# Two graph layers on one core: a pause in the first gathers, weight stages later, six last rows in one root

## The chip, the cores and the metric

The kernel runs on one core of one Trainium2 chip. The metric is the device time of one launch in microseconds (us), the median of several runs. TensorE multiplies and transposes, VectorE, ScalarE and GpSimd compute on tiles, SyncE issues most of the transfers, and GpSimd issues the indirect ones (gathers and scatters by an index column).

## What is computed

`x` is 50000 x 256 in float32. There are 12500 edges `(src, dst)`, sorted by `dst`. Two attention layers follow one another, each with a residual sum and a layer norm:

```python
x = layernorm(x + L0(x, edges))
x = layernorm(x + L1(x, edge_attr, edges))

# L0: 4 heads of 64
h = x @ W
e = leaky(h[src] @ a_src + h[dst] @ a_dst)
alpha = softmax of e over the edges with one dst
out = segment_sum(alpha * h[src], dst) @ W_out

# L1: 4 heads of 32
m = x @ W_n2m.T;  q, k, v from m;  e from edge_attr
alpha = softmax of q[dst] . (k[src] + e) over one dst
out = segment_sum(alpha * (v[src] + e), dst)
x_r = m @ Wskip.T + bskip
beta = sigmoid([out, x_r, out - x_r] @ Wbeta.T)
out = (beta * x_r + (1 - beta) * out) @ W_m2n.T
```

Most nodes have no incoming edge. For them both layers reduce to a function of their own row.

## The kernel before

The program has two kinds of work. **Node steps** (`Nodes`, 196 tiles of 256 rows) treat every row as if it had no edge: load, statistics, first norm, transpose (L741), product with the folded weights `m_ext` (L751), gated update (L777), squares (L716), root on GpSimd (L673, L678), final scaling (`Nodes.scale`: L688 on VectorE or L690 on ScalarE) and store (L658). **Edge work** goes over 100 tiles of 125 edges in five passes: `Score` gathers the rows of src and dst (L831) and projects them (L854 transposes, L864 and L866 products), `soft1` is a softmax over segments, `Gather` sums messages, `Message` builds keys, values and scores of the second layer, `soft2` is its softmax, and `Output` sums the second messages, applies the gate and the norm and scatters the rows over the output.

**Order of the work.** There is one plan, a list of pairs (part, step). Every engine goes through the same list and emits its own instructions of each pair, so each engine's queue is in the order of the plan. `order_of` blends the parts: node steps are spread over the passes by `NODE_SHARE`. `start_of` places the weight stages (`MADE_AT`), the mask stages (`MASKS_AT`) and the positions before given score tiles. In the plan before, node steps 187, 189, 191 and 193 lie among the last message tiles. Step 195 comes before soft2 1, 197 before soft2 4, 199 and 200 between soft2 9 and 10, 201 before soft2 11 and 203 before soft2 14. Node step s holds the scaling of node tile s - 8.

**Start.** `Weights` folds the weight matrices in stages 0 to 4: stage 1 transposes them (TensorE L294 to L297, VectorE L344 to L359), stage 2 multiplies them (L304 to L306, VectorE L363 to L367), stage 3 forms `m_ext` (L310, L311, L371 to L373) and stage 4 removes the means (L315 to L319, L378 to L392). `weights.pe_done` counts the stages that TensorE has finished. Stages 0 and 1 stand ahead of all score steps, stage 2 before score tile 1, stage 3 before tile 2, stage 4 before tile 4. The first mask stage (L449 to L461) stands before tile 1. A node tile is transposed only when stage 4 has made `m_ext` ready. GpSimd issues the two gathers of tile n at plan step n - 5, into a ring of 10 tiles, so it can run ahead of TensorE.

**Output.** Step t turns row tile t (`turn`, L1615), forms its skip product (`skip`, L1622, two tiles later), transposes the message of tile t (L1640), scans it on VectorE (L1712) and multiplies (L1644). The first two row tiles are turned early: tile 0 at t = -3, and at t = -2 come skip 0, turn 1 and skip 1, while the softmax still runs. VectorE finishes a row (L1690, L1702), ScalarE squares it (L1674), VectorE adds epsilon (L1716), GpSimd takes the power -0.5 (L1583), ScalarE scales (L1678) and GpSimd scatters (L1577). `GROUPS` says how many row tiles share one root: two, but one at either end. The tables `WIDENED_AT`, `ROOTS_AT`, `SCALED_AT` and `SCATTERED_AT` are worked out from it.

Of the kernel before, what the change touches and what calls it, by code (L numbers as in the profile page):

```python
# [35 lines left out]
EDGES, TILES = 125, 100  # L36
# [7 lines left out]
NSTEPS = NFULL + 1  # L44
# [5 lines left out]
def at_least(eng, sem, value):  # L50

    if value > 0:
        eng.wait_ge(sem, value)
# [24 lines left out]
def live(s, lag, total):  # L78

    return 0 <= s - lag < total  # L80
# [77 lines left out]
class Head:  # L158
# [53 lines left out]
    def pool(self, pool):  # L212
        c, w = self.c, self.c.scratch
        own = Own(pool, self.pool_done)
        own(pool.memset(c.ident[:, :], 0.0))
        own.done()
        own(pool.affine_select(out=c.ident[:, :], in_=c.ident[:, :], compare_op=ALU.not_equal, fill=1.0,
                               base=0, pattern=[[-1, P]], channel_multiplier=1))
        own(pool.memset(w.zero, 0.0))
        own(pool.memset(w.mean_w, 1.0 / D))  # L220
        own(pool.memset(c.half[:, :], -0.5))
        own(pool.memset(c.half_row[:, :], -0.5))
        own(pool.memset(c.we2[:, :, :], 0.0))
        own(pool.iota(w.posi, [[1, EDGES]], base=1, channel_multiplier=P))
        own(pool.iota(w.basei, [[1, 1]], base=0, channel_multiplier=P))
        own(pool.iota(w.placei, [[1, EDGES]], base=1, channel_multiplier=0))
        own(pool.iota(c.own_pos[:, :], [[P, TILES]], base=0, channel_multiplier=1))
        own.done()
        assert own.n == self.POOL_DONE
        pool.wait_ge(self.columns, 2)  # L230
# [16 lines left out]
    def tensor(self, pe):  # L247
        c, w = self.c, self.c.scratch
        pe.wait_ge(self.pool_done, 2)
        pe.wait_ge(self.dve_done, 7)  # L250
        for k in range(2):
            last = pe.transpose(c.psum[:, 0, k * 256:k * 256 + TILES], w.row[:, k, :], c.ident[0:TILES, 0:TILES])
        last.then_inc(self.turned, 1)


class Weights:

    FIRST, LAST = 0, 5
# [139 lines left out]
class Masks:  # L398

    FIRST, LAST = 0, 5  # L400
# [90 lines left out]
class Positions:  # L491

    FIRST, LAST = 0, 4
# [87 lines left out]
class Nodes:  # L581
# [3 lines left out]
    FIRST, LAST = 0, NSTEPS + 9  # L585
# [212 lines left out]
class Score:  # L798

    A = 5  # L800
    FIRST, LAST = -5, TILES + 2
# [20 lines left out]
    def pool(self, pool):  # L822
        c, R = self.c, self.c.R

        def emit(t):
            if live(t, -self.A, TILES):
                n = t + self.A
                at_least(pool, self.turned, n - R + 1)
                at_least(pool, self.kept[n % R], 16 * (n // R))
                for side, col in ((1, c.src_col), (0, c.dst_col)):  # L830
                    pool.indirect_dma_start(out=c.ring[:, n % R, side, :], out_offset=None, in_=self.x,  # L831
                                            in_offset=bass.IndirectOffsetOnAxis(ap=col[:, n:n + 1], axis=0)).then_inc(self.gathered[n % R], 16)
        return emit
# [62 lines left out]
class Finder:  # L896
# [3 lines left out]
    FIRST, LAST = 0, TILES // 4 + 1  # L900
# [98 lines left out]
class Softmax:  # L999

    PARTS = (0, 10, 40, TILES)
    FIRST, LATER, LAST = 0, 17, 19
# [178 lines left out]
class Gather:  # L1181

    A = 4
    FIRST, LAST = -4, TILES + 5
# [100 lines left out]
class Message:  # L1285

    A = 7
    B = 4
    PICKED = 5
    FIRST, LAST = -8, TILES + 3  # L1290
# [218 lines left out]
        return emit  # L1509


GROUPS = (1, 1) + (2,) * 48 + (1, 1)
GROUP_AT = [sum(GROUPS[:g]) for g in range(len(GROUPS) + 1)]
GROUP_OF = [g for g, size in enumerate(GROUPS) for _ in range(size)]
WIDENED_AT, ROOTS_AT, SCALED_AT, SCATTERED_AT = {}, {}, {}, {}
_at = 0
for _g, _size in enumerate(GROUPS):
    _last = GROUP_AT[_g] + _size - 1
# [8 lines left out]
class Output:  # L1527

    A = 5
    HELD = 10  # L1530
    EARLY = 4
    FIRST_ROWS = 2
    FIRST, LAST = -5, TILES + 11
    PAIRS = ((0, 1), (2, 3), (7, 4))

    def __init__(self, nc, c, ctx, out, masks, nodes, message, weights):
        self.c, self.out, self.masks, self.nodes, self.message, self.weights = c, out, masks, nodes, message, weights

        def sb(name, shape, dt=F32):
            return ctx.enter_context(nc.sbuf_tensor("output_" + name, shape, dt))  # L1540
# [9 lines left out]
        self.ZT = c.AT_flat[:, 0:4 * D].rearrange("p (a n) -> p a n", a=4)  # L1550
        self.va = sb("va", [P, 3, max(GROUPS)])
        self.r = sb("r", [P, 3, max(GROUPS)])
        self.rows_in = c.ring_load + c.ring_out
# [14 lines left out]
    def pool(self, pool):  # L1568
        c = self.c

        def emit(t):
# [7 lines left out]
            for g in ROOTS_AT.get(t, ()):  # L1579
                size = GROUPS[g]  # L1580
                pool.wait_ge(self.widened, g + 1)
# [26 lines left out]
    def tensor(self, pe):  # L1608
        c, ps = self.c, self.c.psum

        def turn(n):
            pe.wait_ge(self.rows_in[n % self.M], self.rows_before[n % self.M] + 16 * (n // self.M + 1))
            at_least(pe, self.zt_ready, n)
            for h in range(2):
                last = pe.transpose(ps[:, 6, h * P:(h + 1) * P], self.row(n)[:, h * P:(h + 1) * P], c.ident[:, :])  # L1615
            last.then_inc(self.z_turned, 1)

        def skip(n):
            pe.wait_ge(self.zt_ready, n + 1)
            at_least(pe, self.z_ready, n - 2)  # L1620
            for h in range(2):
                last = pe.matmul(ps[:, self.PAIRS[n % 3][1], 0:D + 1], self.ZT[:, n % 4, h * P:(h + 1) * P], c.m_ext[:, h, :], start=(h == 0), stop=(h == 1))  # L1622
            last.then_inc(self.skipped, 1)

        def emit(t):
            if t == -3:
                turn(0)
            if t == -2:
                pe.wait_ge(self.nodes.updated, NSTEPS)
                skip(0)  # L1630
                turn(1)
                skip(1)
            if live(t, 0, TILES) and t >= self.FIRST_ROWS:
                turn(t)
            if live(t, 2, TILES) and t - 2 >= self.FIRST_ROWS:
                skip(t - 2)
            if live(t, 0, TILES):
                pe.wait_ge(self.made, t + 1)
                at_least(pe, self.scanned, t)
                pe.transpose(ps[:, 5, 0:P], c.MSG[:, t % G, 0:DM], c.ident[:, :]).then_inc(self.turned, 1)  # L1640
            if live(t, 2, TILES):
                n = t - 2
                pe.wait_ge(self.scanned, n + 1)
                pe.matmul(ps[:, self.PAIRS[n % 3][0], 0:D + 3], self.AG[:, n % 5, :], c.w_out1[:, :], start=True, stop=True).then_inc(self.product, 1)  # L1644
        return emit
# [74 lines left out]
def main_pass(nc, c, io, out):  # L1720

    with ExitStack() as ctx:
# [10 lines left out]
        positions = Positions(nc, c, ctx, masks)  # L1733
        nodes = Nodes(nc, c, ctx, io["x"], out, made, NODE_NORMED, NODE_SCALED)
        assert TILES % c.R == 0
# [49 lines left out]

NODE_SHARE = (74, 10, 66, 45, 10)
NODE_NORMED = ["A" if 74 <= s < 84 or s >= 186 else "AD"[s % 2] if s >= 84 else "D" for s in range(NSTEPS)]
NODE_SCALED = ["AD"[s % 2] if s < 66 else "A" for s in range(NSTEPS)]

MESSAGES_BEGIN = ((3, 1), (1, 1), (1, 1), (1, 1))  # L1790

# [32 lines left out]
    return plan  # L1824


MADE_AT = (-5, -5, 1, 2, 4)
MASKS_AT = (1, 6, 8, 10, 12)
POSITIONS_AT = (14, 16, 18, 20)
NODES_FROM, FINDER_FROM = 2, 22  # L1830
# [2 lines left out]
def start_of(score, finder, nodes, made, masks, positions):  # L1833


    before = {}
    for at, part in ((MADE_AT, made), (MASKS_AT, masks), (POSITIONS_AT, positions)):
        for t, entry in zip(at, part):
# [106 lines left out]
```

## Time and profile before

| | us |
|---|---|
| median of 3 runs | 1260.95 |
| lowest and highest | 1257.87, 1261.74 |
| the profiled execution | 1271.05 |
| its span, first to last instruction | 1269.3 |
| busy in it: TensorE, VectorE | 1174.8, 1041.8 |
| busy in it: ScalarE, GpSimd | 829.2, 851.0 |
| mean granted TensorE clock | 0.978 |

The span is one traced execution, the median is of runs without a trace. The profiled execution is 10.1 us longer than the median. In the rows PE is TensorE, DVE VectorE, ACT ScalarE, POOL GpSimd and SP SyncE; a q behind the name is the engine's sequencer, which issues transfers. L12 is line 12 of the kernel. Matmuls overlap in their pipeline and their ends are modelled.

### The profile page before, as it was taken

Reading aid. Unit: us, or ns where it says so; the run is one execution under the profiler, and the core shown is the slowest. Engines: PE = TensorE matmul, PEld = TensorE weight load, DVE = VectorE, ACT = ScalarE, POOL = GpSimd, SP = SyncE. Lnnn points to the kernel's source line nnn. Section 1 sums busy time; section 2 is a strip of 40 time slices with the busy share of each in tenths; the row PEclk is TensorE's granted clock in tenths of the full one; section 3 lists DMA queues with packets and bytes.
Section 4 is the critical chain, followed back from the end, with each engine's and each line's share of the span. In section 5 each row is a group of like instructions: output and inputs, shape, how many; then the busy total and the mean of one; then the engine's idle time right before and its main releaser. Section 6 shows DMA issues by size and latency. Waiting matters only on the chain.

```text
span 1269.3 us, 28496 instructions
## 1 busy us (share of the span) xinstructions
PE 1174.8 (93%) x6990; PEld 1024.3 (81%) x6990; DVE 1041.8 (82%) x3799; ACT 829.2 (65%) x2787; POOL 851.0 (67%) x1076
## 2 busy tenths in 40 slices
PE   2899999999998689999999899999999996899995
PEld 2788999988896578788788699989999995688884
DVE  2767776777778799999999889999999987788985
ACT  0366666665666866666666856666665668689996
POOL 6688888888883455555554677767677743278887
PEclk9899999999999899999999999999999998899998
DMA  7578888888884477788877787777777742555652
GB/s 210 164 224 284 270 268 257 270 268 266 262 265 132 134 254 249 244 267 249 259 253 238 220 255 217 217 223 221 206 220 223 224 136 78 158 189 187 185 188 96
DMA packets 208795, 276.99 MB, mean 218 GB/s; under 512 B 40044, under 2 KB 140419, under 8 KB 208633
## 3 DMA queue, kind: packets, MB, share of 16 engines
q1 hardware_dynamic: 187913, 223.83, 56.0%
q0 software_dynamic: 19264, 50.85, 13.5%
q8 instruction: 60, 0.98, 0.3%
q14 instruction: 102, 0.84, 0.2%
q10 hardware_dynamic: 1456, 0.49, 0.2%
HBM read 159.67 MB, written 117.12 MB: 218 GB/s over the span
## 4 chain that ended last, share of the span: by engine, by line
PE 58%; DVE 17%; issue 12%; POOL 7%; ACT 3%; DMA 1%; another core or an unknown queue 1%; SPq 1%; DVEq 0%; POOLq 0%; ACTq 0%
PE banks L751 19%; PE banks L864 7%; PE banks L741 6%; PE banks L1422 4%; POOL out L1577 4%; PE banks L854 3%; PE banks L1254 3%; POOL output_r L1583 3%; DVE AT L1280 3%; PE banks L866 2%; PE banks L1409 2%; PE banks L1427 2%; PE banks L953 2%; PE banks L1247 2%; DVE node_X L777 2%
## 5 line engine op out<-in xcount | busy, mean ns | idle before, releaser
L751 PE MATMUL banks<-m_ext,node_XT 128*128 128x257 f32 x1568 | 376.0, 382 | 0.0
L751 PEld LDWEIGHTS banks<-m_ext,node_XT 128*128 128x128 f32 x1568 | 284.6, 192 | 33.0
L777 DVE SCALAR_TENSOR_TENSOR node_X<-banks,node_be,node_X 128x256 f32<-128x256 f32 x392 | 169.4, 474 | 79.5 <-ACT node_be L703 53.6
L678 POOL TENSOR_TENSOR node_r<-node_vv,half 128x4 f32<-128x4 f32 (+1 forms) x202 | 212.8, 1053 | 17.1 <-POOL node_vv L673 0.3
L709 ACT ACTIVATE node_XT<-banks 128x512 f32<-128x512 f32 x196 | 117.5, 599 | 131.7 <-PE banks L741 126.9
L673 POOL TENSOR_SCALAR node_vv<-node_mv 128x4 f32<-128x4 f32 (+1 forms) x202 | 56.5, 279 | 190.3 <-DVE node_mv L785 173.7
L716 ACT ACTIVATE node_sq<-node_X 128x256 f32<-128x256 f32 x392 | 158.0, 409 | 1.2 <-DVE node_X L777 1.2
L770 DVE BATCH_NORM_STATS2 node_st<-node_X 128x6 f32<-128x256 f32 x392 | 145.4, 412 | 1.3 <-issue 0.5
L690 ACT ACTIVATE node_X<-node_X,node_r 128x256 f32<-128x256 f32 x326 | 146.0, 497 | 0.0
L741 PE MATMUL banks<-ident,node_X 128*128 128x128 f32 x784 | 122.0, 279 | 19.0 <-issue 11.9
L831 POOL DMA_INDIRECT ring<-in_x,src_col x100 | 106.8, 1068 | 26.5 <-issue 14.4
L877 ACT ACTIVATE ST<-banks 128x512 f32<-128x512 f32 x100 | 59.8, 598 | 97.5 <-PE banks L854 40.1
L1345 POOL DMA_INDIRECT ring<-rows,src_pos x100 | 106.2, 1062 | 22.8 <-issue 19.7
L741 PEld LDWEIGHTS banks<-ident,node_X 128*128 128x128 f32 x784 | 95.7, 148 | 31.9 <-issue 16.4
L831 POOL DMA_INDIRECT ring<-in_x,dst_col x100 | 97.0, 970 | 31.4 <-issue 31.1
L1577 POOL DMA_INDIRECT out<-store,last_col x90 | 91.4, 1015 | 23.7 <-issue 23.4
L864 PE MATMUL banks<-wh,ST 128*128 128x260 f32 x400 | 105.9, 387 | 1.5 <-ACT store L886 0.2
L1622 PE MATMUL banks<-m_ext,AT 128*128 128x257 f32 x400 | 106.2, 388 | 0.7 <-ACT AT L1660 0.5
L1422 PE MATMUL banks<-w_kv,ST 128*128 128x256 f32 x400 | 105.0, 385 | 0.3 <-DVE store L1470 0.3
L1254 PE MATMUL banks<-wo,AT 128*128 128x256 f32 x400 | 103.0, 380 | 0.0
L1280 DVE TENSOR_TENSOR_SCAN AT<-MB,AT,banks 128x128 f32<-128x128 f32 x198 | 84.0, 466 | 20.2 <-PE banks L1247 17.1
L1449 ACT ACTIVATE ST<-banks 128x512 f32<-128x512 f32 x100 | 59.3, 593 | 62.9 <-PE banks L1409 54.9
(270 smaller groups left out, 2740.8 us busy)
## 6 DMA issues: line engine op xcount, KB each, us to landing
node_X<-in_x SPq DMA_DIRECT2D x196, 256.0 KB
out<-node_X SPq DMA_DIRECT2D x196, 256.0 KB
ring<-rows SPq DMA_DIRECT2D x210, 128.0 KB
rows<-ring SPq DMA_DIRECT2D x100, 256.0 KB
rows<-ring SPq DMA_DIRECT2D x200, 128.0 KB
MB<-keeps SPq DMA_DIRECT2D x40, 320.0 KB, 4.5
store<-rows SPq DMA_DIRECT2D x90, 128.0 KB
MB<-picks SPq DMA_DIRECT2D x50, 128.0 KB
```

Of the source, the lines that this page charges most:

```text
L678: pool.tensor_tensor(r[:, s % 4, NT * lo:NT * hi], v, self.c.half[:, NT * lo:NT * hi], ALU.pow).then_inc(self.roots, 1)
L690: last = eng.activation(row, row, ACT.Identity, scale=rz)
L716: last = act.activation(self.sq[:, k, :], X[:, n % U, k, :], ACT.Square, scale=1.0 / D ** 0.5, accum_out=self.mv[:, s % 4, 1, k, 1:2])
L741: last = pe.transpose(ps[:, 4, k * D + h * P:k * D + (h + 1) * P], self.X[:, n % U, k, h * P:(h + 1) * P], c.ident[:, :])
L751: last = pe.matmul(ps[:, NT * o + k, 0:D + 1], self.XT[:, o, k * D + h * P:k * D + (h + 1) * P], c.m_ext[:, h, :], start=(h == 0), stop=(h ...
L770: last = dve.bn_stats(st[:, s % 2, k, :], X[:, s % U, k, :])
L777: last = dve.scalar_tensor_tensor(out=X[:, n % U, k, :], in0=ps[:, b + k, 0:D], scalar=self.be[:, n % 4, k:k + 1], in1=X[:, n % U, k, :], ...
L831: pool.indirect_dma_start(out=c.ring[:, n % R, side, :], out_offset=None, in_=self.x, in_offset=bass.IndirectOffsetOnAxis(ap=col[:, n:n + ...
L864: pe.matmul(ps[:, 6, 0:HP], c.ST[:, o, h * P:(h + 1) * P], c.wh[:, h, :], start=(h == 0), stop=(h == 1))
L1254: last = pe.matmul(ps[:, 6 + n % 2, 0:D], c.AT[:, n % 4, h * P:(h + 1) * P], c.wo[:, h, :], start=(h == 0), stop=(h == 1))
L1422: pe.matmul(ps[:, 6, 0:2 * DM], c.ST[:, o, h * P:(h + 1) * P], c.w_kv[:, h, :], start=(h == 0), stop=(h == 1))
L1577: pool.indirect_dma_start(out=self.out, out_offset=bass.IndirectOffsetOnAxis(ap=c.last_col[:, n:n + 1], axis=0), in_=self.row(n), in_offse ...
```

## The change

Four edits.

1. GpSimd waits before it issues the gathers of tile 4 until TensorE has finished weight stage 2. Weight stage 1 moves from the head of the plan to score tile 2, stage 2 from tile 1 to 3, stage 3 from 2 to 4, stage 4 from 4 to 6. The first mask stage thereby comes ahead of weight stage 1.
2. `skip(1)` moves from t = -2 to t = 0, behind the transpose of the first message.
3. The last row tiles 94 to 99 are one group instead of (2, 2, 1, 1): one addition of epsilon, one root over six columns, and their scalings and scatters behind it. The last step index grows by three.
4. Of node tiles 178 to 195, the nine odd ones are scaled on VectorE instead of ScalarE.

```diff
@@ Score.pool
             if live(t, -self.A, TILES):
                 n = t + self.A
+                if n == 4:
+                    pool.wait_ge(self.made.pe_done, 2)
                 at_least(pool, self.turned, n - R + 1)
@@
-GROUPS = (1, 1) + (2,) * 48 + (1, 1)
+GROUPS = (1, 1) + (2,) * 46 + (6,)
@@ class Output
-    FIRST, LAST = -5, TILES + 11
+    FIRST, LAST = -5, TILES + 14
@@ Output.tensor
                 pe.wait_ge(self.nodes.updated, NSTEPS)
                 skip(0)
                 turn(1)
-                skip(1)
@@
                 pe.transpose(ps[:, 5, 0:P], c.MSG[:, t % G, 0:DM], c.ident[:, :]).then_inc(self.turned, 1)
+            if t == 0:
+                skip(1)
@@
-NODE_SCALED = ["AD"[s % 2] if s < 66 else "A" for s in range(NSTEPS)]
+NODE_SCALED = ["AD"[s % 2] if s < 66 or s >= 178 else "A" for s in range(NSTEPS)]
@@
-MADE_AT = (-5, -5, 1, 2, 4)
+MADE_AT = (-5, 2, 3, 4, 6)
```

## Rows read from the trace of the kernel before

**Rows 1.** Windows: length, busy of PE, PEld, DVE, ACT, POOL; granted clock, DMA share, GB/s

```profile
100.00:400.00 300.00, 296.95 (x1896) 268.27 (x1894) 220.11 (x827) 187.26 (x590) 238.37 (x271) 1.00 0.83 260
...
1000.00:1040.00 40.00, 39.80 (x270) 36.87 (x269) 36.85 (x162) 25.47 (x74) 23.36 (x31) 1.00 0.58 177
...
1055.00:1067.00 12.00, 9.54 (x51) 7.49 (x50) 9.17 (x25) 12.00 (x40) 5.70 (x9) 1.00 0.23 86
...
1067.00:1081.00 14.00, 4.59 (x23) 3.20 (x23) 11.64 (x35) 10.99 (x30) 5.84 (x9) 0.69 0.35 117
1081.00:1093.00 12.00, 9.32 (x31) 6.80 (x31) 6.13 (x15) 4.27 (x14) 0.00 (x0) 0.65 0.57 174
...
1101.00:1256.00 155.00, 152.41 (x832) 126.66 (x830) 137.77 (x418) 138.53 (x653) 128.54 (x139) 1.00 0.55 176
```

**Rows 2.** Timeline, 10 to 45 us: start, duration, what; idle before and releaser

```profile
10.88 4.77 SPq L193 DMA_DIRECT2D store<-in_dst  x2
...
15.68 0.95 POOL L831 DMA_INDIRECT ring<-in_x,dst_col  x1 [0.30 <-issue]
...
20.26 2.93 PE L304 MATMUL banks<-store 128*128 128x128 f32 x12 [1.86 <-DVE store L353]
...
23.97 0.75 PE L306 MATMUL banks<-store 64*128 64x128 f32 x2
...
28.18 0.94 POOL L831 DMA_INDIRECT ring<-in_x,dst_col  x1 [0.30 <-issue]
...
32.05 0.42 DVE L363 COPY store<-banks 128x256 f32<-128x256 f32 x1 [11.85 <-remote]
32.11 0.60 ACT L877 ACTIVATE ST<-banks 128x512 f32<-128x512 f32 x1 [13.08 <-remote]
...
33.98 2.08 PE L310 MATMUL banks<-w_out,store 128*128 128x257 f32 x4 [7.45 <-DVE we L367]
...
43.61 0.42 DVE L378 SCALAR_TENSOR_TENSOR store<-store,banks 128x257 f32<-128x257 f32 x1 [3.71 <-PE banks L319]
```

**Rows 3.** The chain that ended last, 20 to 54 us

```profile
20.21 11.82 another core or an unknown queue
...
52.95 0.66 PE banks L741 x4
```

**Rows 4.** DMA issues of 0 to 16 us: count, KB each, us to landing

```profile
wh<-in_L_gnn_W SPq DMA_DIRECT2D x2, 128.0 KB, 3.8
```

**Rows 5.** Timeline at the beginning of the output, 1083 to 1090 us

```profile
1083.24 0.63 PE L1615 MATMUL banks<-ident,ring 128*128 128x128 f32 x2
...
1084.35 1.98 PE L1622 MATMUL banks<-m_ext,AT 128*128 128x257 f32 x4 [0.47 <-ACT AT L1660]
...
1086.90 0.42 DVE L1712 TENSOR_TENSOR_SCAN S<-MB,banks 128x128 f32<-128x128 f32 x1 [2.92 <-PE banks L1640]
...
1089.18 0.30 PE L1640 MATMUL banks<-ident,MSG 128*128 128x128 f32 x1 [1.17 <-DVE S L1712]
```

**Rows 6.** The end: timeline, and the roots by shape (busy, mean ns, idle before)

```profile
1256.42 0.48 DVE L1702 SCALAR_TENSOR_TENSOR store<-banks,output_gates,store 128x256 f32<-128x256 f32 x1
...
L1583 POOL TENSOR_TENSOR output_r<-output_va,half_row 128x2 f32<-128x2 f32 x2 | 1.5, 738 | 0.0
...
L1583 POOL TENSOR_TENSOR output_r<-output_va,half_row 128x1 f32<-128x1 f32 x2 | 1.2, 588 | 0.1
...
1266.49 0.98 POOL L1577 DMA_INDIRECT out<-store,last_col  x1 [0.30 <-issue]
```

**Rows 7.** Timeline: a scaling on VectorE, and the engines around steps 193 to 201

```profile
97.02 0.61 DVE L688 TENSOR_SCALAR node_X<-node_X,node_r 128x256 f32<-128x256 f32 x2
...
1050.63 1.10 PE L1422 MATMUL banks<-w_kv,ST 128*128 128x256 f32 x4 [0.34 <-DVE store L1470]
...
1060.08 0.16 DVE L764 SCALAR_TENSOR_TENSOR node_nb<-node_mv,node_r 128x2 f32<-128x2 f32 x1
...
1075.33 1.65 DVE L777 SCALAR_TENSOR_TENSOR node_X<-banks,node_be,node_X 128x256 f32<-128x256 f32 x4
```

## The prediction

> **What bounds the kernel now.** I read the stages first [rows 1]. Each row gives the length of a stretch, then each engine's busy time. In the score stage TensorE is busy 297.0 of 300 us, in the output stage 152.4 of 155 us. There a tile costs TensorE's time and nothing else, so what shifts the beginning of such a stage shifts its end. TensorE is not the limit between 1055 and 1093 us, in the last node steps and the second softmax: ScalarE is busy 12.00 of 12 us, then VectorE 11.64 of 14, then TensorE runs at a granted clock of 0.65, between its two levels. The change works in four places outside the flat stages, and each is read in the timeline or the chain.
>
> At the start [rows 2] one thing stands out. TensorE's second weight stage ends at 23.97 + 0.75 = 24.72 us, yet VectorE takes up its result (L363) only at 32.05, after 11.85 us idle, and ScalarE its next tile (L877) at 32.11. The profile names no engine as the releaser ("remote"). The chain [rows 3] has the same hole, 11.82 us from 20.21, of which 4.5 us are the weight matmuls; 7.3 us are a stall. All through it GpSimd's first 18 gathers are in flight: the last is issued at 28.18, with 0.94 us each and a gap of 0.30. The weight stages stay on the chain until the second node tile is transposed, at 52.95 [rows 3].
>
> The sum is made against the profiled execution, 1271.05 us (span 1269.3 and 1.75 around it). It is 10.1 us above the median of the runs, 1260.95. That matters below: the stall of 7.3 us may be part of the difference. I carry differences in us over to the median. A measurement of this kernel can tell about 0.3%, 3.8 us, from no change.
>
> **Part 1, pause and later weight stages.** The order becomes: first score tiles, then VectorE's first mask step, then weight stage 1 (before tile 2), stage 2 (before 3), stage 3 (before 4), stage 4 (before 6). GpSimd stops after eight gathers (the eighth is issued at 15.68 [rows 2]) until stage 2 is done. Nothing waits behind it but its own ten gathers and the first node roots.
>
> Step by step. The mask step needs the short dst loads, whose issue ends at 10.88 + 4.77 = 15.65 [rows 2]. With the 3.8 us that a measured load took to land [rows 4] that is 19.4. It lasts 2.0 us (an estimate from its 12 short operations after 33.95 in the timeline; I bound it by 1.5 and 2.5). Stage 1 on VectorE, 2.8 us after its transposes as before, then ends at 24.3. Stage 2 takes TensorE 20.26 to 24.72, 4.46 us [rows 2], so it ends at 28.8. If nothing holds that signal up, VectorE copies until 30.7, stage 3 (2.08 us and 0.85 more on TensorE, from 33.98 to 36.9 before [rows 2]) ends at 33.7. GpSimd issues tile 4 from 28.8 to 31.3, it lands about 2.5 us later (an estimate; bounds 1.5 and 5), tile 5 at 36.3. Stage 4 begins on TensorE at 38.0 and lasts 2.3. VectorE's part, 3.9 us from 43.61, now runs from 40.3 to 44.2. The masks and the second node's normalization then follow as before (49.50 to 52.90, 3.4 us). So the second node tile is transposed at 47.5 instead of 52.95 [rows 3]: **-5.5 us**. The gathers had a lead of about 17 us over their use and keep about 10, enough, since the later ones come at the old pace. Bounds: -9 (the whole stall, and some of TensorE's idle time behind it) and +1.8, which is what the same schedule costs if 7.3 us of stall are there again, or were never there in a run without the profiler. My value lies nearer the first, since the signal that came late came when the gathers' traffic had drained.
>
> A rule speaks against this. The Trainium skill, "SBUF — State Buffer", section "SBUF: two separate sides", says that engine ports and DMA ports are disjoint and that neither kind of traffic slows the other; by it fewer gathers in flight free no engine, and the start would come out at +1.8. The rows [2] show only that the stall and the gathers coincide, so I keep this as a rival.
>
> **Part 2, second skip product behind the first message.** Before, TensorE's order is: transpose row 1 until 1083.87, skip product 1 from 1084.35 for 1.98 us, the first message behind it, and VectorE's first scan at 1086.90, idle 2.92 us before it [rows 5]. Now the message, made by 1083.8, follows the transpose at 1083.87, and the scan starts at 1084.6, 2.3 us earlier. The product moves into the time in which VectorE scans and takes its reciprocal (0.88 us), and is still paid: 1084.35 to 1086.33. The second message is next on TensorE, then the second scan at 1086.8, the third message at 1087.4 instead of 1089.18 [rows 5]: **-1.8 us**. It is then TensorE that is late, no longer VectorE. ScalarE's copy of row 1 was ready at 1084.31, nothing on it is queued behind. Bounds: 0 (rows 4 and 5 are loaded from 1083.97 on and could be late) and -2.3.
>
> **Part 3, six rows in one root.** Before, rows 94 to 99 have four roots. GpSimd is full from 1256 on and its last scatter ends at 1266.49 + 0.98 = 1267.47. A root is 0.59 us for one column and 0.74 for two [rows 6]; 0.15 us for each further column gives 1.35 for six. Row 99 is finished on VectorE at 1256.42 + 0.48 = 1256.9 [rows 6]. Its square now follows at once, since ScalarE no longer scales rows 94 and 95 in between: 1257.5, widened by 1257.8, root until 1259.2. Then six scatters: 0.19 + 1.04, and five at 0.97 + 0.30, 7.6 us. End at 1266.7: **-0.75 us**. The scaling, 0.51 each, hides under the scatters. What was saved (three roots, 2.1 us less 0.6) is mostly given back, since five scatters now wait for row 99. Bounds: +0.3 (square where it was, at 1258.5) and -1.3.
>
> **Part 4, nine node tiles scaled on VectorE.** Two scalings took 0.61 us on VectorE [rows 7] against 0.90 on ScalarE. Steps 187 to 193 lie in the message stage, where ScalarE has slack; one of them, at 1048.7, stood before a copy for which TensorE waited 0.34 us [rows 7]: -0.3. Step 195 falls ahead of two long scans. The shift of the next norm came at 1060.08, 0.2 us before ScalarE wanted it [rows 7], so 0.61 costs +0.4. In the same steps ScalarE is full, but dropping 0.9 there gains nothing: its next copy also waits for transposes that end in the same instant. Steps 199 and 201 fall between the second pair of scans and the run over the tiles: VectorE runs without a gap from 1074.7, with its four node updates from 1075.33 to 1076.98 [rows 7], and everything to the first message waits behind it: +1.2. Steps 197 and 203 fall into idle time of VectorE, covered by TensorE and by ScalarE's last copy. Sum **+1.3 us**. Bounds: -1.5 (two of the 0.77 us gaps of TensorE before the node transposes closed) and +5.5 (nine times 0.61, no cover).
>
> **Sum.** -5.5 - 1.8 - 0.75 + 1.3 = -6.75 us, 1264.3 for a profiled execution and **1254.2** against the median.
>
> **Rivals.** *The stall is not the gathers'.* It may belong to the profiled execution, whose 10.1 us over the median leave room for it, or come again at 28.8 and now hold GpSimd as well. For: the profile names no releaser, and TensorE-bound stages leave little room for 10 us elsewhere. Against: both readers woke just as the first gathers had drained. The start is then +1.8, and 1260.95 + 1.8 - 1.8 - 0.75 + 1.3 = 1261.5, no change. This is also what the rule of the page above would give.
>
> *VectorE becomes the bound.* It is 36.85 of 40 us busy in the message stage [rows 1]. If the four scalings there (2.4 us) and the two I count as covered (1.2) lie open, and the start gains nothing, the time is 1261.5 + 3.6 = 1265.1, slower. It decides from the point where TensorE waits for VectorE's normalized rows in that stage; before, it did so once in 40 us, for 0.2. Against: 3.15 us of slack there for 2.4 of work.
>
> *The pause does more.* The whole stall goes, TensorE's idle time after it closes, the parts at the output reach their lower bounds: -9 - 2.3 - 1.3 + 1.3 = -11.3, 1249.6.
>
> **The numbers.** Forecast 0.42, no stall to win 0.37, VectorE 0.13, more 0.08. The likeliest case alone reaches from 1251 to 1257.5. With the neighbours the range is 1250 to 1263; it leaves out about 2 in 10, most of the slower case and the end of the best one. A part of the forecast (0.02) falls short of 3.8 us, so faster 0.48, within 0.3% 0.38, slower 0.14.
>
> **What would show it.** Right: L363 starts within 0.3 us of the end of L306, and the second node transpose near 47.5; GpSimd's ninth gather starts near 29; the first output scan starts 0.8 us after the end of the row 1 transpose, and L1640 stands before the second L1622; one root of 128x6 near 1.35 us, then six scatters at 1.27. Part 4: L688 between L1164 and L1107, and the first message as much later. Wrong: a wait of several us before L363 again, TensorE idle on gathers between 30 and 45, or idle gaps of TensorE in front of L1407 in the message stage. If a profiled execution gains 7 us while the timed runs do not, the stall was the profiler's.

## The result, and the profile after

The changed kernel takes 1270.48 us (median of 5 runs, 1268.19 to 1271.38), against 1260.95 before: ratio 1.0080, 95% interval 1.0066 to 1.0093. Forecast was 1254.2, in a range up to 1263. The change costs 9.5 us, and the sign was wrong. A later series of the same kernel gave 1269.93 against 1261.21 (1.0060, 1.0046 to 1.0074), that is 8.7 us by the medians. The ratios are not quotients of the medians: they stand for 10.1 and 7.6 us. So the loss is known to about 2 us.

One trap first. The traced execution after has a span of 1269.6 us, the one before 1269.3 us: laid side by side, the two traces show no loss. The trace of before was 10 us longer than its timed runs, the trace after is not. So the first run below takes the trace of before again, and all comparisons further down are with that one (span 1256.4).

The long stages look as before [rows 1]. Windows of the kernel after, columns as in [rows 1]:

```profile
88.00:388.00 300.00, 297.66 (x1901) 269.45 (x1900) 220.42 (x816) 191.35 (x589) 242.98 (x280) 1.00 0.84 264
...
1068.00:1082.00 14.00, 4.92 (x24) 3.21 (x22) 11.46 (x35) 10.21 (x28) 5.97 (x9) 0.76 0.32 106
1082.00:1092.00 10.00, 7.96 (x30) 5.79 (x31) 6.79 (x21) 2.85 (x9) 0.00 (x0) 0.65 0.61 201
...
1100.00:1255.00 155.00, 153.29 (x838) 127.52 (x836) 138.82 (x418) 138.77 (x654) 127.91 (x140) 1.00 0.55 176
```

TensorE is full in the score and output stages, as it was. The change must be read where stages begin. The timeline of the kernel after at the start, to be held against [rows 2, 3]:

```profile
15.77 0.94 POOL L833 DMA_INDIRECT ring<-in_x,dst_col  x1 [0.30 <-issue]
...
17.76 0.35 DVE L449 CAST store<-store 100x1 f32<-100x1 int32 x3 [5.76 <-DMA store<-in_dst]
...
23.93 1.60 PE L304 MATMUL banks<-store 128*128 128x128 f32 x12 [1.05 <-DVE w_out L359]
...
26.42 0.42 DVE L363 COPY store<-banks 128x256 f32<-128x256 f32 x1 [1.60 <-PE banks L306]
...
26.66 0.94 POOL L833 DMA_INDIRECT ring<-in_x,src_col  x1 [9.95 <-PE banks L306]
...
33.67 0.66 PE L856 MATMUL banks<-ident,ring 128*128 128x128 f32 x4 [1.12 <-DMA ring<-in_x,dst_col]
...
38.89 0.26 POOL L673 TENSOR_SCALAR node_vv<-node_mv 128x2 f32<-128x2 f32 x1
...
39.99 0.73 DVE L791 TENSOR_SCALAR node_X<-node_X,node_mv,node_r 128x256 f32<-128x256 f32 x2 [8.01 <-POOL node_r L678]
40.64 0.42 DVE L378 SCALAR_TENSOR_TENSOR store<-store,banks 128x257 f32<-128x257 f32 x1
...
42.49 0.66 PE L741 MATMUL banks<-ident,node_X 128*128 128x128 f32 x4 [2.91 <-DVEq L385]
...
48.10 1.12 PE L741 MATMUL banks<-ident,node_X 128*128 128x128 f32 x4 [3.29 <-DVE node_X L791]
```

The order that I had predicted is there: mask step at 17.76 (I said 19.4), stage 2 at VectorE at 26.42, right behind L306, no stall, and the second node tile transposed at 48.10 (I said 47.5). That last agreement is luck. Weight stage 2 took TensorE 2.5 us (23.93 to 26.39) instead of the 4.46 of my sum and ended 2.4 us before my 28.8, and what was gained there was lost again in the middle. GpSimd stands still for 9.95 us, then issues its ten gathers, and only then comes to the first node root, at 38.89. Next in VectorE's order stands the normalization L791, which needs that root: 8.01 us idle ahead of it. L378, the uptake of the fourth weight stage, is queued behind it. TensorE pays at the node transposes: it waits 2.91 us for the first, at 42.49, and 3.29 us for the second. For gathers it waits only 1.9 us (0.76 at 30.68, 1.12 at 33.67).

### The profile page after: what moved, and what is told of

It is laid out like the page before. It is cut to its first block, busy times and chain, and to the rows that moved or that the text cites. A ratio compares the mean times of both kernels' runs of the same rounds, so it can differ in the third digit from the quotient of the medians.

```text
span 1269.6 us, 28487 instructions
## 1 busy us (share of the span) xinstructions
PE 1173.7 (92%) x6990; PEld 1023.7 (81%) x6990; DVE 1050.4 (83%) x3814; ACT 827.8 (65%) x2769; POOL 845.7 (67%) x1073
## 4 chain that ended last, share of the span: by engine, by line
PE 56%; DVE 16%; issue 12%; POOL 9%; ACT 4%; DMA 3%; SPq 1%; ACTq 0%; DVEq 0%; POOLq 0%
PE banks L751 18%; PE banks L866 6%; PE banks L741 5%; PE banks L1424 5%; POOL out L1579 4%; PE banks L1256 3%; PE banks L856 3%; POOL output_r L1585 3%; DVE AT L1282 3%; PE banks L1411 2%; PE banks L868 2%; PE banks L1429 2%; PE banks L955 2%; PE banks L1249 2%; POOL ring L833 2%
## 5 line engine op out<-in xcount | busy, mean ns | idle before, releaser
L678 POOL TENSOR_TENSOR node_r<-node_vv,half 128x4 f32<-128x4 f32 (+1 forms) x202 | 209.6, 1038 | 17.1 <-POOL node_vv L673 0.3
L690 ACT ACTIVATE node_X<-node_X,node_r 128x256 f32<-128x256 f32 x308 | 138.0, 496 | 15.0 <-POOL node_r L678 14.9
L833 POOL DMA_INDIRECT ring<-in_x,src_col x100 | 110.6, 1106 | 36.3 <-issue 13.3
L791 DVE TENSOR_SCALAR node_X<-node_X,node_mv,node_r 128x256 f32<-128x256 f32 x250 | 91.3, 407 | 39.4 <-POOL node_r L678 39.2
```

Source lines behind the costliest of these rows:

```text
L678: pool.tensor_tensor(r[:, s % 4, NT * lo:NT * hi], v, self.c.half[:, NT * lo:NT * hi], ALU.pow).then_inc(self.roots, 1)
L690: last = eng.activation(row, row, ACT.Identity, scale=rz)
```

## The experiments

Times are medians against runs of the unchanged kernel made alongside. "Lag" is how much later TensorE transposes score tile 49 than in the new trace of before, where that is at 191.0 us: from tile 49 to the last tile it changes by 0.4 us at most. Five kernels below leave the start as it was; their tile 49 stands at -0.3 to +1.6 against the same trace, so a single lag is good to about 1 us. It tends to come out too large, since the trace it is measured against is of an execution 2.7 us under the median of its runs.

**The kernel before, again, and the change cut in two.** The first has no edit.

> The kernel before, unchanged, traced and timed once more. Theory A (the stall of 7.3 us behind weight stage 2 does not belong to the executions that were timed): median 1261, ratio 1.000 within 0.002, and either the trace again shows VectorE waiting about 12 us before L363 while the timed executions lie 8 to 10 us below the traced one, or this trace lacks the stall and its own time is then near 1261. Theory B (the stall is in every execution and the loss comes from elsewhere): the trace shows the wait of about 12 us again and its time is near the timed ones, so the first trace's 10 us over the median came from somewhere else.

Measured: 1260.9 us against 1260.54, and the profiled execution took 1258.23. Its timeline (TensorE, VectorE, GpSimd at the start):

```profile
20.14 2.93 PE L304 MATMUL banks<-store 128*128 128x128 f32 x12 [1.86 <-DVE w_out L359]
...
24.68 0.42 DVE L363 COPY store<-banks 128x256 f32<-128x256 f32 x1 [4.60 <-PE banks L306]
...
31.11 0.23 POOL L673 TENSOR_SCALAR node_vv<-node_mv 128x2 f32<-128x2 f32 x1 [1.71 <-DVE node_mv L785]
...
34.17 0.42 DVE L378 SCALAR_TENSOR_TENSOR store<-store,banks 128x257 f32<-128x257 f32 x1 [2.24 <-PE banks L319]
...
43.39 0.66 PE L741 MATMUL banks<-ident,node_X 128*128 128x128 f32 x4 [0.96 <-DVE node_X L791]
```

L363 starts at 24.68, behind L306, not at 32.05 [rows 2]. The stall that carried my forecast belonged to one execution. The score tiles come 9.4 us earlier than in the first trace, which is nearly all of its 10.1 us over the median. The normal second transpose is at 43.39, so 48.10 in the kernel after is a loss of 4.7 us, not the gain of 4.9 that it is against 52.95.

```diff
+                if n == 4:
+                    pool.wait_ge(self.made.pe_done, 2)
-MADE_AT = (-5, -5, 1, 2, 4)
+MADE_AT = (-5, 2, 3, 4, 6)
```

> The kernel before with the pause in the gathers and the later weight stages alone. Theory A (no stall in timed executions, so this part only delays the gathers and the weights): slower by 6 to 10 us, 1267 to 1271, nearly the whole loss. Theory B (the loss comes from the scaling on VectorE or from the output): 1253 to 1262, faster or the same, as the prediction's -5.5 us or its bound +1.8 has it.

Measured: 1267.6, +7.1 us (1.0063, 1.0050 to 1.0077); lag 7.3.

The complement, parts 2, 3 and 4 on the kernel before:

> The kernel after without its first part: skip product, last group and scaling on VectorE together. Theory A: 1259 to 1262, the prediction's sum of these three is -1.25 us. Theory B: 1266 to 1270, most of the loss.

Measured: 1260.37, -0.2 us (1.0000, 0.9991 to 1.0009). So the start is the loss, and the other three gain nothing together. Next, the start without its pause, the line MADE_AT alone:

> The kernel before with the weight stages later and no pause in the gathers. If the pause itself costs (the lead of the gathers is lost and TensorE waits for rows from tile 4 on): 1260 to 1263, that is, little of the loss. If the later weight stages cost (the first node tile is turned later): 1266 to 1270, most of it.

Measured: 1262.9, +2.4 us (1.0024, 1.0014 to 1.0034); lag 2.6. Its timeline:

```profile
36.85 0.43 DVE L378 SCALAR_TENSOR_TENSOR store<-store,banks 128x257 f32<-128x257 f32 x1 [3.31 <-PE banks L319]
...
44.32 0.66 PE L741 MATMUL banks<-ident,node_X 128*128 128x128 f32 x4 [3.29 <-DVE node_X L791]
```

Tile 1 is transposed 7.2 us earlier than before, tile 3 2.4 us earlier, and then the gain is gone: the fourth stage stands behind tile 5 on TensorE and reaches VectorE 2.7 us later than before, its four us of work go ahead of the node normalizations, and TensorE waits 3.29 us for one. By the third node tile the kernel is 2.6 us late and stays so.

**Each part alone.** The pause alone, two lines:

> Only the wait of GpSimd before the gathers of tile 4; the weight stages stand where they stood before. Theory A (GpSimd's own order: it stands still, and the ten gathers behind the wait keep the first node roots back; with the early stages the second weight stage ends about 24.5 us, so GpSimd should lose about 8 us instead of 10): +3 to +6 us against before, the first node root near 37 us instead of 31.1, the transposes of node 0 late, and from tile 8 on every score tile later by that amount. Theory B (the pause hurts only together with the later stages, which move VectorE's work behind it): within 1 us of before. If fewer gathers in flight free other engines at all, tiles 1 to 3 come earlier than before (24.6, 28.0, 29.7 us).

Measured: 1265.59 against 1261.42, +4.2 us (1.0038, 1.0025 to 1.0051); lag 5.4. GpSimd in it:

```profile
25.05 0.94 POOL L833 DMA_INDIRECT ring<-in_x,src_col  x1 [8.38 <-PE banks L306]
...
37.53 0.26 POOL L673 TENSOR_SCALAR node_vv<-node_mv 128x2 f32<-128x2 f32 x1
```

Two things follow. Tiles 1 to 3 stand within 0.2 us of before. So holding back the seven gathers that were issued between 17 and 25 us freed no other engine. And the loss does not stand at the first nodes (+0.3 us at both, the kernel had that much room there) but grows later: +2.0 at tile 9, +2.8 at tile 20, +5.5 at tile 25, mostly where TensorE waits for a node normalization. Why it must come shows in the new trace of before, waits of GpSimd from 14 to 140 us (total, times, longest):

```profile
POOL ring L831 <- issue: 16.5, 57, 0.3
POOL ring L831 <- POOL node_r L678: 2.5, 13, 0.2
POOL node_vv L673 <- DVE node_mv L785: 1.7, 1, 1.7
POOL ring L831 <- PE banks L854: 0.5, 2, 0.3
POOL ring L831 <- DVE node_X L791: 0.3, 1, 0.3
```

The first two rows are the 0.2 to 0.3 us that stand between its own instructions in any case. In 126 us it waits for another engine for 1.7 + 0.5 + 0.3 = 2.5 us at most. The last 0.8 of that are three gaps of the usual size, so 1.7 may be the better count. An engine with so little slack can't stand still for 8 to 10 us without passing most of it on.

The three other parts, each with its own lines of the diff and nothing else:

> Only the second skip product moved behind the first message. By my prediction -1.8 us; by the run without the start, whose output stage gained 1.9 us on TensorE in the first five messages, -1.5 to -2; rival (the gain was another part's): 0.

Measured: 1258.47, -3.0 us (0.9980, 0.9971 to 0.9989).

> Only the last six rows in one root. By my prediction -0.75 us (bounds +0.3 and -1.3). By the run without the start, in which the last scatters lost 0.4 us against the scatters in mid-stage: +0.4. Either lies near what the measurement can tell; the trace decides: length of the 128x6 root, and the time from the last message's transpose to the last scatter's end against before.

Measured: 1260.87, -0.6 us (0.9994, 0.9984 to 1.0004).

> Only the nine node tiles scaled on VectorE. By my prediction +1.3 us. By the run without the start, in which the message stage lost 1.0 us from tile 73 on and the last node steps 0.3: +1 to +2. Rival (those losses come with the clock's moments of change, which shift from run to run): within 0.5.

Measured: 1262.23, +0.8 us (1.0006, 0.9997 to 1.0014).

**How much pause.** The pause alone, moved to the gathers of tile 6:

```diff
-                if n == 4:
+                if n == 6:
```

> The pause alone, placed before the gathers of tile 6 instead of 4, so that GpSimd stands still from about 22.1 us to 24.7 us, 2.7 us instead of 8.4. Theory A (GpSimd has almost no slack in the score stage, so that its standstill is paid beyond some 3 us of lead): 0 to +0.7 us. Theory B (the wait as such costs, or the traffic that it bunches up): +3 to +5 us as with the pause before tile 4.

And before tile 4, but until the third weight stage:

```diff
-                    pool.wait_ge(self.made.pe_done, 2)
+                    pool.wait_ge(self.made.pe_done, 3)
```

> The pause alone before the gathers of tile 4, but released by the third weight stage (its product ends at 28.2 us instead of 24.6), so that GpSimd stands still for about 11.9 us instead of 8.4. Theory A (each further us of standstill is paid in full): +3.5 us more than the pause alone, so +8 to +9 us against before. Theory B: the same +4.8 as the shorter pause.

Measured: 1261.69, +0.5 us (1.0002, 0.9993 to 1.0010), and 1269.0, +7.8 us (1.0058, 1.0045 to 1.0071). One line of each timeline, first the short pause, which was longer than the 2.7 us I had reckoned, as the second stage ended later in this execution:

```profile
25.81 0.95 POOL L833 DMA_INDIRECT ring<-in_x,src_col  x1 [4.07 <-PE banks L306]
```

then the long one:

```profile
28.36 0.94 POOL L833 DMA_INDIRECT ring<-in_x,src_col  x1 [11.53 <-PE banks L311]
```

Put in order, with the two kernels that follow further down and have both pause and late stages:

| standstill of GpSimd | lag of tile 49 | kernel |
|---|---|---|
| 4.07 | 1.2 | pause at tile 6 |
| 8.38 | 5.4 | pause alone |
| 9.95 | 7.8 | after |
| 9.97 | 7.3 | start only |
| 11.24 | 8.6 | after, without the scaling |
| 11.53 | 9.1 | pause until stage 3 |
| 11.69 | 9.2 | after, again |

In every row the lag is the standstill less 2.2 to 3.0 us, close to the 1.7 to 2.5 us of slack counted above, given that a lag is good to about 1 us. The first row, 1.2, is within what kernels with an unchanged start show. The late stages appear nowhere as a term of their own: 11.53 us of standstill with the stages in place gave 9.1, and 11.69 with late stages gave 9.2. The reading that fits is two delays of one stream, of which the larger counts.

**The fourth stage's place.**

```diff
-MADE_AT = (-5, -5, 1, 2, 4)
+MADE_AT = (-5, 2, 3, 4, 5)
```

> The later weight stages without the pause, but the fourth before tile 5 instead of 6. Theory A (the +2.4 us of the later stages is the fourth stage's place alone: it reached VectorE at 36.85 instead of 34.17 us, and the node normalizations queue behind its 3.9 us there): VectorE takes it up at about 34.8, the transposes of node 2 stand at +0.5 us instead of +2.6 against before, and the time is within 1 us of before. Theory B (what counts is that the first stages are late, tile order or the masks): still +2 to +3 us.

Measured: 1260.86 against 1261.21 (0.9991, 0.9980 to 1.0001). L378 stands at 35.52, the third node tile at +1.3 us instead of +2.6, tile 49 at +2.0. The time fits the first theory; the trace shows half of the effect left at the third node tile, in an execution that took 1262.70 us, 1.8 over the median of its runs, and whose mask step began late (20.49 us). The direction is shown, the share isn't.

**What the parts make together.** Parts 2 and 3:

> Parts 2 and 3 without the start and without the scaling, the version that should beat both kernels. Each alone measured -2.5 and -0.75 us (the latter within what can be told). If they add up: -3 us against before (ratio 0.9975). Rival: they don't add up, since the start without its parts (all three together) measured 0: then within 1 us of before.

Measured: 1258.58, -2.6 us (0.9982, 0.9973 to 0.9990). With the scaling added they gave -0.2, so the scaling costs about 2.4 us beside them (by the ratios 2.3, give or take 1.6), though it measured +0.8 alone. What the scaling and the pause cost inside the whole change:

> The whole change but part 4. Theory A (the parts add up): start +7.1 us and parts 2 and 3 -2.3 give +4.8 against before, near 1266; the scaling then costs 4.7 us inside the whole change, and the trace should show it between the 187th and 203rd node step. Theory B (the parts don't add up because the late start takes their gain): as the whole change, +9 to +10.

Measured: 1267.12, +5.9 us (1.0052, 1.0038 to 1.0066).

> The changed kernel unchanged. Its time should come out at +9.5 us again (ratio 1.008). If the wait of VectorE for the short load of picks at the beginning of the message stage (2.44 and 0.65 us in the first profile, 0.2 to 0.5 in six others) is the change's own, it stands here again; if it was one execution's, it is under 0.6 us.

Measured: 1269.93, +8.7 us (1.0060, 1.0046 to 1.0074). VectorE's wait for picks is 0.8 us here: most of the 3.1 us belonged to one execution.

> The whole change but the pause. If the parts add up: later stages +2.4 us and the three other parts 0 give +2.4 against before. If the loss that the parts alone don't explain is the later stages' with the scaling: +5. In either case GpSimd's first node root near 29.4 us.

Measured: 1262.89, +1.7 us (1.0016, 1.0007 to 1.0025).

By the first pair the scaling costs 2.8 us in place, by the second the pause 7.0. The first isn't clear of noise: by the ratios it is 1.0 us, give or take 2.5. The second is: 5.5, give or take 2.1, and tile 49 stands 7.1 us earlier without the pause. So the scaling's cost is taken from the traces below. For the pause, the mask step now stands ahead of the signal that releases GpSimd, and it waits for a load. In the kernel after, again:

```profile
19.69 0.35 DVE L449 CAST store<-store 100x1 f32<-100x1 int32 x3 [6.82 <-DMA store<-in_dst]
...
28.34 0.94 POOL L833 DMA_INDIRECT ring<-in_x,src_col  x1 [11.69 <-PE banks L306]
```

The load came 1.9 us later than in the first trace and the standstill was 1.7 us longer. So the pause in the whole change is not the one I costed: the late stages lengthen it, from 8.38 us to between 9.95 and 11.69.

For the scaling, VectorE before the first output message, after without part 4:

```profile
1073.61 1.65 DVE L777 SCALAR_TENSOR_TENSOR node_X<-banks,node_be,node_X 128x256 f32<-128x256 f32 x4
1075.18 0.34 DVE L1109 TENSOR_TENSOR_SCAN run<-along,banks 4x100 f32<-4x100 f32 x1
```

and with it (the kernel after, again):

```profile
1076.23 0.87 DVE L777 SCALAR_TENSOR_TENSOR node_X<-banks,node_be,node_X 128x256 f32<-128x256 f32 x2
1077.02 0.61 DVE L688 TENSOR_SCALAR node_X<-node_X,node_r 128x256 f32<-128x256 f32 x2
1077.54 0.87 DVE L777 SCALAR_TENSOR_TENSOR node_X<-banks,node_be,node_X 128x256 f32<-128x256 f32 x2
1078.33 0.61 DVE L688 TENSOR_SCALAR node_X<-node_X,node_r 128x256 f32<-128x256 f32 x2
1078.85 0.34 DVE L1109 TENSOR_TENSOR_SCAN run<-along,banks 4x100 f32<-4x100 f32 x1
```

From the four updates to L1109 it is 1.57 us without and 2.62 with: +1.05. Three stretches that hold nothing but node steps and their stage give the whole, each in three traces with the scaling (three parts together; after; after again) and two without (parts 2 and 3; after without scaling). From the key and value product (L1422) of message tile 49 to that of tile 99 it is 159.3 to 159.7 against 158.5 to 158.6; from there to the last node transposes 14.50 against 14.12; and from these to the first output scan 20.53 against 20.03. The first difference is 0.7 us between the two kernels with the old start and 1.2 between the two with the new one. In all, the scaling costs 1.6 to 2.1 us.

**A version that beats both.**

```diff
-MADE_AT = (-5, -5, 1, 2, 4)
+MADE_AT = (-5, 1, 2, 3, 4)
```

on top of parts 2 and 3, without pause and scaling.

> Parts 2 and 3 with the weight stages at tiles 1, 2, 3 and 4: the first three one tile later than before, the fourth where it stood. Theory A (only the fourth stage's place sets when the node chain begins): the transposes of node 2 within 0.5 us of before, and the time that of parts 2 and 3 alone, -2.3 us against before. Rival (the earlier first tiles are a gain that reaches the end): -4 us or more. Rival (a late third stage pushes the fourth): the transposes of node 2 at +1 to +2, and the time near before's.

Measured: 1255.84 us (1253.7 to 1256.95) against 1261.21, ratio 0.9955 (0.9941 to 0.9968): 5.4 us faster than the kernel before, and 2.7 better than parts 2 and 3. Its timeline:

```profile
21.05 1.60 PE L304 MATMUL banks<-store 128*128 128x128 f32 x12 [0.23 <-DVE w_out L359]
...
31.01 0.42 DVE L378 SCALAR_TENSOR_TENSOR store<-store,banks 128x257 f32<-128x257 f32 x1 [1.91 <-PE banks L319]
...
40.20 0.66 PE L741 MATMUL banks<-ident,node_X 128*128 128x128 f32 x4 [0.96 <-DVE node_X L791]
```

The theory that only the fourth stage's place matters falls. The fourth stage stands before tile 4 in both, yet it reaches VectorE at 31.01 instead of 34.17, and the second node transpose is 3.2 us earlier. TensorE has tile 0's products to do while VectorE prepares stage 2 (idle 0.23 instead of 1.86 us before L304), and the same twelve matmuls take 1.60 instead of 2.93 us. Part of what I expected of the late stages is thus real; the change put them one or two tiles too far, and spoiled it with the pause.

## Why the prediction was wrong, step by step

**Part 1, the step that decided.** Two steps failed. The first: I took the 7.3 us stall [rows 2, 3] as a cost of every execution that fewer gathers would remove. I had the contrary as a rival, with a chance of 0.37, and named its best evidence, the 10.1 us between profiled execution and median. The new trace shows the stall gone with not a line changed, and the pause alone moves tiles 1 to 3 by at most 0.2 us. Without the stall my sum gave the start +1.8, and the late stages alone measured near that, +2.4. The rest is the pause, which had no term of its own. That is the second step that failed: "The gathers had a lead of about 17 us over their use and keep about 10, enough". The gathers' lead did nearly hold: TensorE waited 1.9 us for them in the kernel after and not at all in the pause alone. But the engine's own lead is what counts: in its order the node roots stand behind the ten gathers, and with 1.7 to 2.5 us of slack in 126 it doesn't catch up. I had even written that nothing waits behind the pause "but its own ten gathers and the first node roots", and priced neither. So the rival with +1.8 for the start was priced too low as well: measured +7.1. The page of the Trainium skill, "SBUF — State Buffer", section "SBUF: two separate sides", which I held against the change, says that neither kind of traffic slows the other; the pause alone agrees with it, tiles 1 to 3 being within 0.2 us of before.

**Part 2** was right. With the move and without the scaling, the first output scan starts 20.03 us after the last node transposes in all four traces; with neither it starts 21.7 to 22.4 us after them in nine. That is -1.7 to -2.3, where I said -2.3. The third message, by which I priced the part at -1.8, stands at 22.30 to 22.54 against 23.99 to 24.62, -1.5 to -2.3. Over the first ten rows it grows further, to -2.2 or -2.4 against the new trace of before. The runs measured -3.0 with an interval that reaches from -1.4 to -3.7. One thing that I hadn't priced goes the same way. In the new trace of before TensorE is busy 1.16 of the 3.30 us from 1073.0, and then the granted clock, which had come back to 1.00, is 0.50 again from 1076.3 to 1079.7. In parts 2 and 3 it is 1.00 from 1075.3 to 1090.0. How much of the excess this is, no run shows. The timeline after, against [rows 5]:

```profile
1086.28 0.47 PE L1641 MATMUL banks<-ident,MSG 128*128 128x128 f32 x1
...
1086.85 0.42 DVE L1715 TENSOR_TENSOR_SCAN S<-MB,banks 128x128 f32<-128x128 f32 x1 [0.43 <-PE banks L1641]
1086.96 2.08 PE L1624 MATMUL banks<-m_ext,AT 128*128 128x257 f32 x4 [0.21 <-ACT AT L1663]
```

The product lies beside the scan, as predicted.

**Part 3** failed in one gap. The end of the kernel after, against [rows 6]:

```profile
1256.36 0.48 DVE L1705 SCALAR_TENSOR_TENSOR store<-banks,output_gates,store 128x256 f32<-128x256 f32 x1
...
1257.67 1.36 POOL L1585 TENSOR_TENSOR output_r<-output_va,half_row 128x6 f32<-128x6 f32 x1 [0.43 <-DVE output_va L1719]
...
1260.38 1.04 POOL L1579 DMA_INDIRECT out<-store,last_col  x1 [1.35 <-ACT store L1681]
...
1266.83 0.97 POOL L1579 DMA_INDIRECT out<-store,last_col  x1 [0.30 <-issue]
```

The root of six columns takes 1.36 us (I said 1.35). But from its end to the first scatter I put 0.19, the gap that stands there when earlier rows are ready to go. Now no row is: the first one has still to be scaled, and the gap is 1.35. That the scaling hides under the scatters holds for five of six. So -0.75 becomes about +0.4. The traces show just that: from the start of the last L1705 (L1702 before) to that of the last scatter it is 10.45 to 10.49 us in all eight traces with the group and 10.08 to 10.13 in all ten without. The timed runs can't tell this from nothing.

**Part 4** had the sign right and was too small. I said +1.3; the stretches give 1.6 to 2.1, medians of pairs 2.4 and 2.8. The term that was missed is the message stage: I gave it -0.3 for one copy that would come sooner, and it lost 0.7 to 1.2 between tiles 49 and 99. My rival "VectorE becomes the bound" had this mechanism and more of it than there is. At step 195 I said 0.4, and the stretch from tile 99 to the last node transposes lost 0.4. At steps 199 and 201 I said 1.2; VectorE loses 1.05 there, of which 0.5 arrives at the first output scan.

**The sum.** Start +7.1, parts 2 and 3 -2.6, scaling +2.4: +6.9, against 9.5 and 8.7 in two series. The difference of about 2 us is no more than the intervals of these terms allow together. The length of the pause, which hangs on when one load lands, may be part of it: the standstill was 9.97 us in the trace of the start alone, 9.95 and 11.69 in two of the whole change. That it is the cause isn't shown.

## What to carry over

When a traced execution is longer than the timed runs by more than they scatter, take a second trace before explaining anything in it: here a hole of 7.3 us that no engine released belonged to that execution. Before making an engine wait, add up its waits for others over the stretch that follows; here nearly all that the pause was longer than that sum came through, though that engine's transfers were far ahead of their use. And price everything that stands behind the pause in that engine's order, the small operations that others wait for above all.

## What was not expected of the hardware

The stall named "remote" in the first trace held VectorE and ScalarE at once for 7.3 us. None of the other 17 traces has a wait with that name. The name tells little, though: the same trace gives it to ten further waits of ScalarE between 49 and 374 us, of 1.6 to 3.0 us each and nine of them in front of L877, where the new trace names TensorE. What held the two engines stays open.

Where the message stage begins, the granted clock falls to 0.50 after TensorE has waited for rows (busy 1.49 of the 4 us before 718.00 in the kernel before, again), and the moment at which it comes back differs between kernels that are the same up to there. Windows of the kernel before, again:

```profile
722.00:724.00 2.00, 2.00 (x14) 1.84 (x14) 1.72 (x7) 1.46 (x7) 1.68 (x4) 1.00 0.83 244
```

and of parts 2, 3 and 4 together, with the same order of work there:

```profile
722.00:724.00 2.00, 2.00 (x11) 2.00 (x11) 1.18 (x5) 0.34 (x2) 1.72 (x2) 0.52 0.92 247
```

Both are busy throughout, one at the level of 2.4 GHz, the other at nearly that of 1.2. From the first message tile to the fiftieth the second takes 159.3 us and the first 158.0, with nothing to do with its edits. Differences of one to two us between single traces must therefore be read within a stage and not across its beginning; the account of the scaling above is made that way.

The twelve matmuls of L304 took 2.93 us in the kernel before, where TensorE had been idle 1.86 us ahead of them, and 1.60 in the kernels with late stages, where it had been idle 0.23 to 1.10, with a granted clock of 1.00 shown over both stretches. It is not these alone: the four transposes of a score tile took 1.06 us at 17.21 in the new trace of before and 0.60 at 28.01, in the trace after 1.09 at 16.59 and 0.60 already at 21.06. My sum took the long duration over to the new place, where it was 2 us too much. The profile doesn't show why.
